# Attention scores on two fp32r pieces in the two 64-row halves of the array, in place of three bf16 pieces over 96 rows

## The reference

```python
def _mha(x, w_in, b_in, w_out, b_out):
    qkv = x @ w_in.T + b_in
    q, k, v = jnp.split(qkv, 3, axis=-1)
    ...
    scores = jnp.einsum('bhqd,bhkd->bhqk', q, k) / jnp.sqrt(jnp.asarray(hd, x.dtype))
    attn = jax.nn.softmax(scores, axis=-1)
    out = jnp.einsum('bhqk,bhkd->bhqd', attn, v)
    ...
...
for lvl in range(LEVELS):
    outs.append(_mha(query[:, ::2 ** lvl, :], in_proj_w[lvl], in_proj_b[lvl], out_w[lvl], out_b[lvl]))
current = outs[-1]
for lvl in range(LEVELS - 2, -1, -1):
    current = _upsample_linear(current, outs[lvl].shape[1]) @ up_w[lvl].T + up_b[lvl] + outs[lvl]
```

## Time and profile before

| | us |
|---|---|
| median of 3 runs | 4458.91 (4449.41 to 4462.23) |
| the profiled execution | 4468.91 |
| its span | 4467.1 |
| busy TensorE matmul (PE) / weight load (PEld) | 3904.1 / 2152.1 |
| busy VectorE (DVE) / ScalarE (ACT) / GpSimd (POOL) | 2665.8 / 2448.1 / 1160.8 |

### The profile page before, as it was taken

One profiled execution on the slowest core, in us unless ns is written; L12 is line 12 of the kernel. 1 busy time (PEld: TensorE's weight loads), 2 busy tenths in 40 slices (PEclk: granted clock), 3 DMA queues, 4 the chain that ended last, 5 costly groups with the idle time before them and its releaser, 6 DMA issues. The chain is left out here.

```text
span 4467.1 us, 69697 instructions
## 1 busy us (share of the span) xinstructions
PE 3904.1 (87%) x20881; PEld 2152.1 (48%) x20881; DVE 2665.8 (60%) x4841; ACT 2448.1 (55%) x3163; POOL 1160.8 (26%) x1000
## 2 busy tenths in 40 slices
PE   4599989989989988998998998963999999999998
PEld 2233333333333333333333333323887877877787
DVE  2287777777777777777777777836333333333333
ACT  1376756756756756665675675643444444434343
POOL 4334433424423433433443342220000000000000
PEclk7799999999999999999998999976999999999999
DMA  5443343334344344343334334115000000000000
GB/s 179 101 84 85 97 83 91 92 84 92 91 77 90 101 84 84 101 86 78 84 96 85 91 91 79 29 55 208 10 11 11 20 11 11 20 11 11 10 20 10
DMA packets 308843, 307.47 MB, mean 69 GB/s; under 512 B 75168, under 2 KB 285280, under 8 KB 308192
## 3 DMA queue, kind: packets, MB, share of 16 engines
q1 hardware_dynamic: 299200, 293.59, 26.7%
q10 hardware_dynamic: 9216, 8.39, 0.5%
HBM read 202.28 MB, written 96.47 MB: 67 GB/s over the span
## 5 line engine op out<-in xcount | busy, mean ns | idle before, releaser
L736 ACT ACTIVATE a_probs<-a_p_s 128x1024 f32<-128x1024 f32 x1360 | 1323.1, 1021 | 734.2 <-PE a_p_s L992 725.5
L810 DVE TENSOR_REDUCE a_part_max<-a_p_m 128x1 f32<-128x512 f32 x2048 | 1337.9, 680 | 436.7 <-PE a_p_m L1007 431.9
L1007 PE MATMUL a_p_m<-a_k_st,a_q_st 96*128 96x512 bf16 (+2 forms) x2944 | 1024.5, 380 | 252.2 <-DVE a_part_max L810 153.7
L1387 PE MATMUL p_h<-f_h_hi,f_w_hi 128*128 128x512 f32 x2048 | 811.4, 396 | 40.0 <-issue 35.4
L992 PE MATMUL a_p_s<-a_q_st,a_k_st 98*128 98x512 bf16 (+2 forms) x2944 | 830.7, 370 | 17.6 <-ACT a_probs L736 12.0
L1007 PEld LDWEIGHTS a_p_m<-a_k_st,a_q_st 96*128 96x128 bf16 x2944 | 260.9, 98 | 1174.9 <-DVE a_part_max L810 779.1
L1387 PE MATMUL p_h<-f_h_lo,f_w_hi 128*128 128x512 f32 x2048 | 807.2, 394 | 1.9 <-issue 1.9
L1024 PE MATMUL a_p_o<-a_probs,a_v_aug 128*17 128x512 f32 (+2 forms) x5888 | 740.6, 583 | 0.8 <-ACT a_probs L736 0.8
L1356 DVE TENSOR_TENSOR f_h_lo<-f_h_f,f_h_hi 128x512 fp32r<-128x512 f32 x256 | 177.2, 692 | 721.8 <-ACT f_h_hi L1269 721.8
L810 DVE TENSOR_REDUCE a_row_max<-a_p_m 128x1 f32<-128x512 f32 (+2 forms) x672 | 440.3, 680 | 187.3 <-PE a_p_m L1007 182.1
L1267 ACT ACTIVATE f_h_f<-p_h,f_sc 128x512 f32<-128x512 f32 x256 | 176.6, 690 | 582.5 <-PE p_h L1387 582.5
(11 more groups left out here) (113 smaller groups left out, 4584.8 us busy)
## 6 DMA issues: line engine op xcount, KB each, us to landing
qk_scratch<-a_qk_bf SPq DMA_DIRECT2D x96, 384.0 KB, 2.4
a_w_lo<-wqkv_inner SPq DMA_DIRECT2D x32, 768.0 KB, 4.3
a_q_st<-qk_scratch SPq DMA_DIRECT2D x192, 128.0 KB, 6.1
a_k_st<-qk_scratch SPq DMA_DIRECT2D x192, 128.0 KB, 6.4
a_q_st<-qk_scratch SPq DMA_DIRECT2D x336, 64.0 KB, 2.6
a_k_st<-qk_scratch SPq DMA_DIRECT2D x336, 64.0 KB, 2.6
a_a_lo<-a_attn SPq DMA_DIRECT2D x384, 32.0 KB, 2.0
a_o_lo<-wo_inner SPq DMA_DIRECT2D x24, 512.0 KB, 3.5
```

Of the source, the lines that this page charges most:

```text
L736: act.activation(probs[:, s % 2, 2 * p:2 * p + 2, :], p_s[:, 2 * p:2 * p + 2, :], ACT.Exp, scale=HD ** -0.5).then_inc(exp_done.sem, 1)
L810: dve.reduce_max(out, src, AX.X).then_inc(max_read.sem, 1)
L1007: ins = pe.matmul(p_m[:, n % 2, r * size:(r + 1) * size], q_st[0:ROWS, unit.place, j, q * 128:(q + 1) * 128], k_st[0:ROWS, unit.halves[kb] ...
L1387: ins = pe.matmul(out, a, c, start=first and n == 0, stop=last and n == len(terms) - 1)
```

## The change

Queries and keys are cut into two fp32r pieces instead of three bf16 pieces, and three pairs of pieces are multiplied instead of six. A head then needs 48 rows (50 with the two rows of the maximum). `k_st` and `q_st` hold two heads side by side: one in partitions 0 to 49, one in 64 to 113. A max or score matmul is issued on a 64x128 part of the array, at row 0 or row 64. The bytes per element double, the tiles stay as large as before.

The order in a step is another: the four maxima come as two pairs, each ahead of a score task, and the first score task comes ahead of the value task. GpSimd has one operation per `proj` instead of three. A `neg` is four DMAs instead of two, and `neg_cut` has one buffer instead of two.

```diff
-K_PIECES = (0, 0, 0, 1, 1, 2)
-Q_PIECES = (0, 1, 2, 0, 1, 0)
+K_PIECES = (0, 0, 1)
+Q_PIECES = (0, 1, 0)
+HALF = 64
...
+BANK_HEAD = (0, 2, 1, 3)
...
-        p.append((m // 4 - LEAD + (0, .05, .3, .6)[m % 4], "max", m))
+        p.append((m // 4 - LEAD + (0, .02, .42, .44)[m % 4], "max", m))
...
-        p += [(s + .4, "score", 2 * s), (s + .7, "score", 2 * s + 1), (s + (2.1 if s < STEPS - 1 else 1.3), "value", s)]
+        p += [(s + .1, "score", 2 * s), (s + .5, "score", 2 * s + 1), (s + (2.25 if s < STEPS - 1 else 1.25), "value", s)]
...
-        k_st = sb("k_st", [128, HALVES, HG, W], BF16)
+        k_st = sb("k_st", [128, HALVES, HG // 2, W], F32R)
...
SyncE, neg:
-                            for i in range(2):
-                                sp.dma_start(q_st[ROWS + i:ROWS + i + 1, place, :, :],
-                                             neg_bf[0:HG, n % 2, i, :]).then_inc(neg_placed[n % 2].sem, 16)
+                            for e in range(2):
+                                for i in range(2):
+                                    at = HALF * e + ROWS + i
+                                    sp.dma_start(q_st[at:at + 1, place, :, :].bitcast(F32),
+                                                 neg_cut[2 * e:2 * e + 2, i, :].bitcast(F32)).then_inc(neg_placed[n % 2].sem, 16)
...
GpSimd, proj:
-                            pool.tensor_tensor(out=rest, in0=rest, in1=bf[:, 0, :], op=ALU.subtract)\
-                                .then_inc(qk_rest_done.sem, 1)
...
-                            pool.tensor_copy(bf[:, 1, :], rest).then_inc(qk_b.sem, 1)
...
-                            pool.tensor_tensor(out=bf[:, 2, :], in0=rest, in1=bf[:, 1, :], op=ALU.subtract)\
-                                .then_inc(qk_c.sem, 1)
+                            pool.tensor_tensor(out=lo, in0=lo.bitcast(F32), in1=hi, op=ALU.subtract).then_inc(qk_c.sem, 1)
...
ScalarE, proj and neg:
-                            qk_c.wait(act, it, n)
+                            stored[n % 2].wait(act, it, STORED[n] - len(PROJ[n]))
...
-                            neg_b.wait(act, it, n)
-                            neg_placed[n % 2].wait(act, it, n // 2)
+                            neg_placed[(n - 1) % 2 if n else 0].wait(act, it, (n + 1) // 2)
...
TensorE, score and max:
-                            for j in (2 * p, 2 * p + 1):
+                            for j in (2 * p + 1, 2 * p):
+                                low = HALF * (j % 2)
...
-                                    ins = pe.matmul(p_s[:, j, i * size:(i + 1) * size], k_st[0:ROWS + 2, unit.halves[half], j, key:key + 128],
-                                                    q_st[0:ROWS + 2, unit.place, j, i * size:(i + 1) * size], start=True, stop=True)
+                                    ins = pe.matmul(p_s[:, j, i * size:(i + 1) * size], k_st[low:low + ROWS + 2, unit.halves[half], p, key:key + 128],
+                                                    q_st[low:low + ROWS + 2, unit.place, p, i * size:(i + 1) * size], start=True, stop=True)
...
+                            low = HALF * (m % 2)
...
-                                ins = pe.matmul(p_m[:, n % 2, r * size:(r + 1) * size], q_st[0:ROWS, unit.place, j, q * 128:(q + 1) * 128],
-                                                k_st[0:ROWS, unit.halves[kb], j, key:key + size], start=True, stop=True)
+                                ins = pe.matmul(p_m[:, n % 2, r * size:(r + 1) * size], q_st[low:low + ROWS, unit.place, pair, q * 128:(q + 1) * 128],
+                                                k_st[low:low + ROWS, unit.halves[kb], pair, key:key + size], start=True, stop=True)
```

More of the change, by code:

```diff
@@ L166, in _, with max_column @@
                 sp.sem_clear(s.sem)
+def max_column(turn, e):
+    q, s = divmod(turn, 2)
+    return q * HG + 2 * e + s
 class Signal:
@@ L364, in attention @@
         row_max = sb("row_max", [128, RING, NQ, HG])
-        neg_f = sb("neg_f", [HG, W])
-        neg_bf = sb("neg_bf", [HG, 2, 2, W], BF16)
+        neg_cut = sb("neg_cut", [HG, 2, W], F32R)
         raw = sb("raw", [128, 2, W])
@@ L400, in attention @@
         qk_mm, qk_read, qk_hi = sig("qk_mm", NP), sig("qk_read", NP), sig("qk_hi", NP)
-        qk_rest_done, qk_b, qk_c = sig("qk_rest_done", NP), sig("qk_b", NP), sig("qk_c", NP)
+        qk_c = sig("qk_c", NP)
         stored = [sig(f"stored{i}", sum(len(ps) for ps in PROJ[i::2]), 16) for i in range(2)]
-        stacked = [sig(f"stacked{n}", 2 * len(K_PIECES), 16) for n in range(len(STACKS))]
+        stacked = [sig(f"stacked{n}", 4 * len(K_PIECES), 16) for n in range(len(STACKS))]
         v_mm, v_done = sig("v_mm", len(V_PAIRS)), sig("v_done", len(V_PAIRS))
@@ L406, in attention @@
         neg_mm, neg_read, neg_hi, neg_b = sig("neg_mm", NU), sig("neg_read", NU), sig("neg_hi", NU), sig("neg_b", NU)
-        neg_placed = [sig(f"neg_placed{i}", (NU + 1 - i) // 2, 32) for i in range(2)]
+        neg_placed = [sig(f"neg_placed{i}", (NU + 1 - i) // 2, 64) for i in range(2)]
         score_mm, exp_done = sig("score_mm", 2 * STEPS), sig("exp_done", 2 * STEPS)
@@ L614, in _ @@
                 pool.wait_ge(set_done.sem, 1)
-                pool.memset(k_st[ROWS:ROWS + 2, :, :, :], 1.0).then_inc(set_done.sem, 1)
-                pool.wait_ge(set_done.sem, 2)
+                for e in range(2):
+                    pool.memset(k_st[HALF * e + 32:HALF * e + 64, :, :, :].bitcast(F32), 1.0).then_inc(set_done.sem, 1)
+                    pool.wait_ge(set_done.sem, 2 + e)
                 pool.memset(minus_half[:, :], -0.5).then_inc(set_done.sem, 1)
-                pool.wait_ge(set_done.sem, 3)
+                pool.wait_ge(set_done.sem, 4)
                 xt_summed.open(pool)
@@ L1490, in program @@
 def program(nc, xt, xtok, wqkv, wo, cols, rows, wf, scales, ident, out):
-    scr = [nc.dram_tensor(f"qk_scratch{i}", (2, 3, E, tokens(i)), BF16, kind="Internal").ap() for i in range(LEVELS)]
+    scr = [nc.dram_tensor(f"qk_scratch{i}", (2, 2, E, tokens(i)), F32, kind="Internal").ap() for i in range(LEVELS)]
     d75s, d25s = [nc.dram_tensor(name, (tokens(1), E), F32, kind="Internal").ap() for name in ("up_near", "up_far")]
```

75 lines of the change are left out of this document (41 added, 34 removed).

## The result

The changed kernel takes 4808.55 us (median of 4 runs, 4778.77 to 4849.75), beside 4460.57 for the kernel before on the same chip (4449.41 to 4469.34). The ratio is 1.0788, with a 95% interval of [1.0698, 1.0878]. So it is slower, as forecast, but by 348 us and not by about 100, and 19 us beyond the upper end of the range.

A forecast was written before the change was run, and what follows sets the result against it. It took free steps as bound by a TensorE-VectorE ring, heavy steps by TensorE's own sum. 21.1 - 7.7 + 0.8 = 14.2 us per batch, 12.9 after stalls, times 8: +103, forecast 4560 us; range 4390 to 4790.

The forecast's parts named there:

- clock held: Assumption of the forecast (chance 0.50) that TensorE's granted clock stays at full speed, so clock loss costs nothing.
- the heavy step: Step with a large side task, taken as TensorE's own sum: 4.01 us instead of 4.23.
- The ring: TensorE-VectorE dependency loop setting free steps: 3.59 us instead of 3.13, with a score pair and visible loads added.
- The term of 21.1 per batch: Added us per batch from the longer loop: 35 free steps at 0.46 and 15 `neg` steps at 0.33.
- -7.7 per batch: Saving in us over the 35 heavy steps of a batch, 0.22 each.
- Around it: Effects outside the step terms, at `proj`, `neg` and start-up: +0.8 us per batch.
- -5.2 per batch: Saving in us at close projections, where ScalarE no longer waits for GpSimd.
- ScalarE's waits at `neg` for the DMAs: With one `neg_cut` buffer, ScalarE stands 7.8 us at `neg` 6, less a lead of about 2: +6 per batch.
- Rival 3: Row halves of a pair do not work side by side: +334 us, about 4790; chance 0.12.
- Rival 4: Longer TensorE idle lowers the clock; a third of 50 steps take 5.1 us: +200, about 4760; chance 0.13.
- 14.2: Added us per batch from all terms, cut to 12.9 because one step in ten stands in a stall.

The follow-up runs named there:

- e14: Kernel before with the new table of places, and ScalarE's read of a side task's bank 0.2 of a step behind it instead of 0.3: 4536.60 us.
- e6: Kernel before (bf16 pieces, no row halves) with only the new table of places: 4600.71 us.
- e5: Changed kernel with ScalarE's read of a side task's bank 0.2 of a step behind it instead of 0.3: 4721.72 us.
- e11: Changed kernel with three extra copies of the second score pair in every step without a heavy side task: 4652.74 us.
- e13: Changed kernel with three extra second score pairs per step without heavy side task, and ScalarE's bank read at 0.2 instead of 0.3: 4558.71 us.
- e9: Changed kernel with both heads of each pair read from the lower half of the array's rows, so pairs run in turn: 5435.47 us.
- e10: Changed kernel with score and maximum matmuls in turn over all 128 rows, maximum rows zeroed and Exp scaled by 0.001: 4731.57 us.
- e8: Changed kernel with the value task cut into two column halves behind successive maxima, places changed and ScalarE's read at 0.15: 5062.11 us.
- e4: Changed kernel with the whole old table of places, keeping fp32r pieces and row halves: 4590.07 us.
- e15: Changed kernel with the old table of places and two extra second score pairs in every step without a heavy side task: 4533.76 us.

## Why the prediction was wrong

The direction was right, and so were the terms of a single step at full clock; the size was not. Two steps of the prediction failed: "clock held", on which the forecast rests, and the heavy step, whose sum has no wait for ScalarE's read. Point by point:

- **The ring**: free steps 3.51 to 3.54 for 3.59; `neg` steps alike. The halves work side by side, and loads behind a wait show 0.11. The term of 21.1 per batch was too large all the same: at full clock and with the read early (e14) the order costs 62 us in all, under 8 per batch, since many free steps are longer than the ring for other reasons (mean 3.49, commonest 3.13, in before).
- **Heavy steps**: alone 3.89 for 4.01, so -7.7 per batch looked safe. It did not come: the mean rose from 4.30 to 4.55. I had followed TensorE and VectorE through the step, and of ScalarE only the waits that fall away. The table moves the first score from 0.4 to 0.1 of a step and leaves ScalarE's bank read at 1.15, so that it falls from ahead of the next `Exp` to behind it. This wait is missing in the sum: 62 us (e6 to e14) to about 100 (after to e5, e11 to e13).
- **Around it**: ScalarE's 19 waits for GpSimd at `proj`, 68.2 us in all before, are gone, as forecast; what that is worth (-5.2 per batch in the sum) no run shows alone. ScalarE's waits at `neg` for the DMAs are 71.9 us, 50.5 of them once in the start-up; the rest, 21.4 in eight batches, is 2.7 per batch and not 6. No run has a second buffer for `neg_cut`.
- **The clock**: this is the step that failed most. The forecast, with its chance of 0.50, put the cost of the clock at nothing ("clock held"). The clock fell to 0.85 of full speed in the attention stage, 18 of some 50 free and `neg` steps of a batch began at 1.2 GHz, and e11 got 164 us back with useless work alone. Rival 3 named the nearest time (4790) with a cause that is excluded, since the halves do work side by side. Rival 4 had the clock, with 4760, at a chance of 0.13, and its sizes came out: 5.1 us for such a step (measured 5.16) in a third of the 50. That its 4760 lies near the measured time is in part luck, since it too lacks the wait for ScalarE's read. Its cause is not enough: it blamed TensorE's longer idle time, but e6 has the longer ring and keeps 0.97, and e9 and e10 idle alike and differ. It also took as a comfort that at the lower clock TensorE fills the step. In e9 it fills the step wholly (5.58 of 5.58) and the clock stays down. What the change takes away is work of the array in rows: a maximum or score matmul used 96 or 98 rows for 0.22, and now two share that many rows for 0.23, so there is half as much of it per step. That fits e6, e9 and e10; e8 shows that it is not the whole rule, and what the rule is stays open.
- **A slip in the sum**: a tenth less than 14.2 is 12.8 and not 12.9, which moves nothing.

The sum by the runs: order at full clock +124 (e6), of which 62 the late read; pieces and halves in the old order +119 (e4), of which some 60 came back with the fill (e15); together 243. The other 105 of 348, with an uncertainty of some 40, appear only when both are there. The new order may make the clock worse (0.87 in e4, 0.85 in after; 14 and 18 cold steps), but this part is what is left over, not shown by a run of its own.

## What to carry to other kernels

Packing small contractions side by side saves array time, and that is a gain only where the array is the bound. Here another engine set the free step; packing left TensorE with less work in its rows, and the granted clock fell. So before halving the rows of matmuls, ask what the granted clock does in stretches with few rows at work, and try it with one run in turn over all rows beside one over half of them. And when tasks are moved in a table of places, follow every engine's list across the step's edge: a task that jumps over another one's fixed place is a new wait for whoever shares its bank.

## What was not expected of the hardware

- The granted clock went with the rows of the matmuls: 0.75 with 48 to 50 rows in turn on half of the array (e9), 0.97 with 128 on all of it (e10), the step's timing at full clock being the same. Between 600 and 2900 us TensorE was busy 97% by its rows in e9 and 91% in e10.
- Once down, it stayed down through steps in which TensorE was busy nearly or wholly all the time (5.08 of 5.16 us in the changed kernel, 5.58 of 5.58 in e9).
- Useless work made the kernel faster: three repeated score pairs in each free and `neg` step, -164 us (e11).
- Two matmuls in different row halves took 0.23 together, with a load of 0.11 visible once per pair.
- Where one half was still taken, the later-issued matmul of a score pair started some 0.25 ahead of its partner (1549.92 and 1550.17).
